# Edge counting: the range entry of the next group is read ahead of the current group's loop

## The reference

```python
edge_index = jnp.stack([src, dst])
xn = _layernorm(x, axis=-1)
deg = jax.ops.segment_sum(jnp.ones((src.shape[0],), x.dtype), dst, num_segments=n)
aggr = jax.ops.segment_sum(h[src], dst, num_segments=n) * inv_deg
```

## Time and profile before

| | us |
|---|---|
| median of 3 runs | 2264.9 |
| lowest and highest run | 2263.97, 2267.33 |
| the profiled execution's own time | 2263.15 |
| its span in the profile | 2261.3 |
| TensorE busy in the span | 2012.4 (89%) |
| VectorE busy in the span | 835.3 (37%) |
| the counting, first half round of keys to last product | 54.8 to 221.8 |

### The profile page before, as it was taken

How to read it: one execution, slowest core, us unless ns; L and a number is a source line. 1 busy time by engine, 2 the same in 40 slices (tenths; PEclk the granted TensorE clock), 3 DMA queues, 4 the chain that set the end, 5 groups by cost and what they waited for, 6 DMA issues and landing times. The chain is left out here.

```text
span 2261.3 us, 27789 instructions
## 1 busy us (share of the span) xinstructions
PE 2012.4 (89%) x9440; PEld 1569.6 (69%) x9441; DVE 835.3 (37%) x1670; ACT 645.5 (29%) x1161; POOL 567.2 (25%) x422
## 2 busy tenths in 40 slices
PE   0767998999999988979989989999799999899992
PEld 0444657888888866768857767888688577678881
DVE  8777611111111134451034336322501442462237
ACT  5722002111111111014146543222131574331110
POOL 3000213232323222215011114433240121163321
PEclk9999799999999999988889989999788899999996
DMA  2010302222230393330000010111000000101111
GB/s 51 1 47 13 139 0 80 88 88 99 77 113 26 129 299 111 107 100 32 1 1 1 1 56 19 38 38 51 22 20 1 0 1 20 38 19 55 39 46 45
DMA packets 55501, 119.55 MB, mean 53 GB/s; under 512 B 6288, under 2 KB 8884, under 8 KB 53594
## 3 DMA queue, kind: packets, MB, share of 16 engines
q1 hardware_dynamic: 55380, 117.95, 15.6%
HBM read 82.82 MB, written 35.11 MB: 52 GB/s over the span
## 5 line engine op out<-in xcount | busy, mean ns | idle before, releaser
L561 PE MATMUL ps<-yT,wslot 128*128 128x500 f32 (+1 forms) x576 | 210.6, 366 | 10.5 <-DVE xm L1535 3.6
L787 PE MATMUL ps<-g,adj 125*125 125x512 f32 x800 | 193.5, 405 | 17.1 <-issue 17.1
L563 PE MATMUL ps<-yT,wslot 128*128 128x500 f32 (+1 forms) x576 | 208.0, 361 | 0.0
L562 PE MATMUL ps<-yT,wslot 128*128 128x500 f32 (+1 forms) x576 | 207.8, 361 | 0.0
L787 PEld LDWEIGHTS ps<-g,adj 125*125 125x125 f32 x800 | 153.0, 192 | 57.6 <-issue 18.4
L1566 POOL TENSOR_TENSOR wslot<-mix_landing,wslot 128x2048 fp32r<-128x2048 f32 x24 | 111.1, 4627 | 197.6 <-ACT wslot L1304 197.6
L1570 POOL TENSOR_TENSOR hidT<-qpT,hidT 128x500 fp32r<-128x500 f32 (+1 forms) x96 | 104.6, 1092 | 197.6 <-DVE hidT L1450 197.6
L358 PE MATMUL ps<-key_hot,row_hot 125*125 125x500 bf16 x430 | 105.3, 385 | 46.5 <-DVE key_hot L328 35.5
L561 PE MATMUL ps<-parts,w 128*128 128x500 f32 (+1 forms) x384 | 136.3, 355 | 6.3 <-DVE bl L904 6.3
L1357 ACT ACTIVATE qpT<-ps,layer_cols 128x500 f32<-128x500 f32 (+1 forms) x96 | 58.3, 609 | 288.8 <-PE ps L563 247.2
L562 PE MATMUL ps<-parts,w 128*128 128x500 f32 (+1 forms) x384 | 136.1, 354 | 0.0
(11 more groups left out here) (254 smaller groups left out, 3721.5 us busy)
## 6 DMA issues: line engine op xcount, KB each, us to landing
mix_landing<-in_L_mix_W SPq DMA_DIRECT2D x16, 1024.0 KB, 5.1
g_dram<-staged SPq DMA_DIRECT2D x40, 256.0 KB, 2.0
u_dram<-staged SPq DMA_DIRECT2D x40, 256.0 KB, 2.0
g_in<-g_dram SPq DMA_DIRECT2D x40, 256.0 KB, 3.6
u_in<-u_dram SPq DMA_DIRECT2D x40, 256.0 KB, 2.7
landing_blocks<-in_L_gnn_Wl SPq DMA_DIRECT2D x8, 1024.0 KB, 5.5
landing_blocks<-in_L_gnn_Wr SPq DMA_DIRECT2D x8, 1024.0 KB, 6.9
adj_dram<-adjT SPq DMA_DIRECT2D x5, 1250.0 KB, 10.6
```

Of the source, the lines that this page charges most:

```text
L561: nc.tensor.matmul(out, lhs_high, rhs_high, start=first, stop=False)
L562: nc.tensor.matmul(out, lhs_high, rhs_low, start=False, stop=False)
L563: return nc.tensor.matmul(out, lhs_low, rhs_high, start=False, stop=last)
L787: last = nc.tensor.matmul(m.ps[0:P, t % 2, :], counts if exact else counts.bitcast(F32), part if exact else part.bitcast(F32), start=(s == ...
```

## The change

On both engines the decoding is taken out of the group's function and handed in. VectorE decodes a turn's first entry at the start of the turn, and then, ahead of each bank's loop, the entry of the next bank; the last bank of a turn decodes nothing. TensorE does the same, with the next entry's load between the opening product and the loop. The entry of a turn's first bank is not read in the turn before, so ahead of the first loop of a turn there are two loads, and ahead of the last one none. Arithmetic, waits and their values stay as they were, and ScalarE, GpSimd and the DMAs are untouched.

```diff
-                def key_hots(turn, bank):
-                    lo, rounds, before = decode(vec, turn * BANKS + bank)
+                def key_hots(turn, bank, entry):
+                    lo, rounds, before = entry
                     with vec.Fori(0, rounds) as j:
...
-                for bank in range(BANKS):
-                    key_hots(0, bank)
+                def turn_hots(turn):
+                    entry = decode(vec, turn * BANKS)
+                    for bank in range(BANKS):
+                        following = decode(vec, turn * BANKS + bank + 1) if bank + 1 < BANKS else None
+                        key_hots(turn, bank, entry)
+                        entry = following
+
+                turn_hots(0)
...
                 with vec.Fori(1, GROUP_TURNS) as turn:
-                    for bank in range(BANKS):
-                        key_hots(turn, bank)
+                    turn_hots(turn)
...
-                def count_group(turn, bank):
+                def count_turn(turn):
+                    entry = decode(pe, turn * BANKS)
+                    for bank in range(BANKS):
+                        entry = count_group(turn, bank, entry)
+
+                def count_group(turn, bank, entry):
                     acc = m.ps[0:P, bank, 0:GW]
-                    lo, rounds, before = decode(pe, turn * BANKS + bank)
+                    lo, rounds, before = entry
                     pe.wait_ge(banks_free, turn * BANKS + bank + 1)
                     nc.tensor.matmul(acc, zeros[:, 0:P], zeros[:], start=True, stop=False)
+                    following = decode(pe, turn * BANKS + bank + 1) if bank + 1 < BANKS else None
                     with pe.Fori(0, rounds) as j:
...
                     nc.tensor.matmul(acc[:, 0:2], zeros[:, 0:P], zeros[:, 0:2], start=False, stop=True).then_inc(group_counted, 1)
+                    return following
```

More of the change, by code:

```diff
@@ L371, in _ @@
                 pe.wait_ge(ranges_ready, 1)
-                for bank in range(BANKS):
-                    count_group(0, bank)
+                count_turn(0)
                 for t in range(T):
@@ L382, in _ @@
                 with pe.Fori(1, GROUP_TURNS) as turn:
-                    for bank in range(BANKS):
-                        count_group(turn, bank)
+                    count_turn(turn)
 def stage_gates_and_first_sum(nc, m, gate_W, gate_b, adj_dram, Wl, Wr):
```

## The result

The changed kernel takes 2268.61 us in the median of 22 runs (2260.63 to 2277.81), the kernel before 2264.02 in 22 runs beside them. The ratio of the two is 1.003, with a 95% interval from 1.0016 to 1.0044: **slower by 0.3%**, 6.8 us (3.6 to 10); the two medians lie 4.6 us apart, inside that interval. One slow run of before, 3035.34 us, is left out of the ratio. Single runs of either kernel scatter by 0.5% about their median, so a difference of this size shows in many runs or in the stage itself, not in one pair of runs.

A forecast was written before the change was run, and what follows sets the result against it. Borders between groups were taken as bound by TensorE's sequencer. Two loads at bank 0 (+0.65 and +3.0), none at bank 4 (-1.5, 0, -0.2) gave about +2.0 us on the 2264.9 median: 2266.9 us, range 2262 to 2271.

The forecast's parts named there:

- What bounds a border: Between groups of the counting: a border costs what TensorE's sequencer needs; single-round first products are 3.57 us apart.
- Part 1: Banks 1 to 3 of every turn: the load moves behind the opening matmul but stays on the path, 0 us.
- Part 2: Bank 0 holds two loads: TensorE 4 x 0.75 = +3.0 us in turns 1 to 4, VectorE +0.65 in turn 0.
- its highest sum: Upper bound over all banks, +4.6 us, with 0.6 for a 902 ns load beside the doubled one and no bank 4 gain.
- Part 3: Bank 4 holds no load: -1.5 us together in turns 0 and 1, net 0 in 2 and 3, -0.2 in 4.
- the gain of 0.44: Bank 4 in turns 2 and 3: TensorE starts at most 0.44 us earlier, then loses it again; net 0.
- 4.7 us at the change of turn: Sign expected in the changed profile: bank 4's to the next bank 0's first product takes 4.7 us, where it was 3.98.
- The sum: All effects on the counting: +0.65 + 3.0 - 1.5 + 0 - 0.2 = +1.95, say +2.0 us.
- rival C: Another clock rhythm: one low-clock stretch more or less, anywhere later, worth up to 3 us; 2270 or 2264, chance 0.07.
- Rival A: Loads leave TensorE's path and VectorE's halves bound the borders: faster, sum -10.5 us, 2254; chance 0.06.
- rival B: A load behind the opening matmul waits until the array drains: 19 x 0.6 = 11.4 us slower, 2278; chance 0.05.

The follow-up runs named there:

- e5: Kernel before, with TensorE loading and decoding every entry twice in turns 1 to 4; ratio to before 1.0086 (1.0055 to 1.0118).
- e6: Kernel before, with turns 1 to 4 written out instead of looped on TensorE and VectorE; ratio to before 0.9982 (0.9956 to 1.0008).
- e8: Kernel before, with TensorE waiting for row_hot once ahead of turns 1 to 4, not in every round; ratio to before 1.0003 (0.9980 to 1.0026).
- e7: Kernel before, with turns 1 to 4 written out and the next entry read ahead through all 25 groups; ratio to before 0.9994 (0.9967 to 1.0022).
- e1: The changed kernel profiled and timed once more with no edit; ratio to the kernel before 1.0028 (1.0008 to 1.0049).
- e2: TensorE's code as in the change, VectorE's as in the kernel before; ratio to the kernel before 1.0027 (1.0005 to 1.0049).
- e12: The changed kernel, with the store of normalised rows held back until eight groups were copied out; ratio to the kernel before 1.0020 (0.9999 to 1.0041).
- e9: The changed kernel, plus five products of zeros behind bank 0's opening product in turns 1 to 4; ratio to the kernel before 1.0009 (0.9991 to 1.0027).
- e10: Kernel before, with turns 1 to 4 written out and one wait for row_hot ahead of them; ratio to before 0.9931 (0.9909 to 0.9953).

## Why the prediction was right, and where it was wrong

The time lay in the range (2268.6 in 2262 to 2271) and 1.7 us above the forecast. The side did not hold: "the same" had 0.81, and the kernel is slower by 0.3%. Slower by more than 0.2% had 0.12; the interval of the measurement, 0.16 to 0.44%, begins just under that line.

- **What bounds a border** was right: TensorE's sequencer. e5 puts a load there and pays it in full, e6 and e8 take steps away and gain, until VectorE's second half bounds every second group of one round.
- **Part 1, nothing at banks 1 to 3,** was right: 3.53 to 3.64 us at full clock, and e7 says the same for all borders. The opening product did move ahead, and nobody was waiting for it.
- **Part 2, bank 0:** +0.75 each was right for turn 2 (0.86) and, with bank 4 in front of it, for turns 3 and 4 (0.8). It was too small for turn 1, 1.1 to 1.6 us, of which 1.35 lie behind the last transpose (3.16 and 3.18 us for 1.83): the long load of 902 ns in the earlier trace rows was taken for a chance that might stand beside the doubled one, while it was the rule for a load beside the store, and both were long. The prediction had these 0.6 us, but in its highest sum only. VectorE's first group was +0.7 for +0.65.
- **Part 3, bank 4:** -0.8 and -0.8 for -0.75 each, 0 in turns 2 and 3 and -0.2 in turn 4, as forecast; the second half waited for at 186.93 is the step that gives the gain of 0.44 back. The profile was to show 4.7 us at the change of turn and shows 5.23: bank 4's product comes 0.44 earlier, so the way from it to bank 0 is that much longer. The text had this gain and its loss, but left it out of that number.
- **The sum** at full clock was +2.0 and measured +2.8 (6.0 less the 3.2 of the clock). The 0.8 is turn 1's: 0.6 by the long load, the rest by where the transposes ended. With the clock, the stage ended 6.0 us later and not 2.
- **The step that failed is rival C.** It named the clock, but placed it anywhere later, took it for chance that no row prices, and gave it 0.07; its sign, a stage that ends within 0.5 us of before while the total moves, looked outside the stage. Its price, up to 3 us, was right. It belonged to the change: the doubled load lengthens TensorE's idle time at four borders, on stretches whose clock was full but whose array was busy for three quarters only (36.15 of 48 us), and the clock fell at two or three of them in each profile of these loads (the change, e1, e2, e12), 3 us in sum. In e9, with the same borders and products in the gap, it fell at none. The page TensorE: Matmul & The Clock Gate of the Trainium skill (What's actually happening), which the prediction cites, has it that activity releases the throttle; e9 agrees with it, while e5, which idles more and kept a full clock from 176 us on, shows that it does not say at which border. Whether the clock holds should have been asked of the very gaps that part 2 makes longer.
- **Rival A** (2254) and **rival B** (2278) both fell. The loads behind the opening product took 0.30 us like the others. The Trainium skill has in Advanced Engine Details and Errata, Sequencer Loop, that other engine instructions can be read and queued while a control instruction executes. The traces do not bear it out for these register loads: the opening weight load stood 0.78 us behind the closing one while the load was between them, and follows it at once in the change (184.45, 184.66) where the load is gone from there.

That the time came out near the forecast is in part luck: the forecast stood on a median of three runs, 2264.9, where 22 runs give 2264.0, and on a sum of 2.0 us where the counting took 6.0.

## What to carry to other kernels

Reading a value ahead can be expected to help only where the sequencer that reads it would otherwise stand still (no run here shows such a place); where it is itself the bound, e7 shows that it neither gains nor costs: count the loads between two pieces of work and not their distance from the use. A prefetch inside a hardware loop that cannot cross the loop's edge doubles the load on one side and drops it on the other, and the two need not cancel: here the doubled one was paid in full at all four turns of the loop, while the saved one was won in two turns (0.8 us each) and met the next bound, VectorE's halves, in the others. And ask of every gap that an edit lengthens on TensorE whether the clock survives it.

## What was not expected of the hardware

- A load to a register takes TensorE 0.30 us, and 0.87 to 0.91 while the store of 2.5 MB runs beside it (e12 moved the store, and the loads were short). Through what the two meet isn't shown.
- At the bank 0 of turn 3 the weight loads of the change are idle for 1.19 us ahead of the opening one and about 1.46 behind it, where it was 1.05 and 0.70 before and is 1.18 and 0.56 in e9. With these gaps the granted clock fell to half at two or three of the four places of each profile; with one load there it never fell in seven profiles, nor at 1.18 and 0.56 in the one of e9.
- Five products of zeros with constant addresses behind the opening one cost the border nothing (5.20 and 5.23 us with them and 5.21 to 5.25 without), where a load with its register steps costs 0.6 to 0.8.
- The rest of the program, the same in all kernels, took from 2027 to 2042 us from profile to profile (2253.0 - 225.6 and 2270.3 - 228.7), twice the change's effect. What sets that was not tried; these two (e9 and the change) also have the least and the most time at half clock behind the counting, 260 and 291 us, but e10 has 289 with 2032 us, so that this is not all of it. Nor was it tried what makes the seven rounds of the first group take 23.7 to 24.0 us in some executions and 24.3 to 24.7 in others.
